# Two passes through a three-batch loop body in place of six written-out batches, on four of five engines

## The reference

```python
x = x + tanh(g_xattn[0]) * xattn(layernorm(x), ctx_512, Wq, Wk, Wv, Wo, bo)
x = x + tanh(g_ffn[0])  * ffn(layernorm(x), gate_w, expert_w, expert_b)

# xattn: 16 heads of 64, keys and values from ctx_512 (8, 512, 128)
scores = einsum('bhnd,bhmd->bhnm', q @ Wq, kv @ Wk) * 64 ** -0.5
out    = einsum('bhnm,bhmd->bhnd', softmax(scores), kv @ Wv) @ Wo + bo

# ffn: softmax router over 8 experts, the two best kept, all experts computed
comb = sum(one_hot(top2(softmax(x @ gate_w.T))) * weight)
out  = sum_e (x @ expert_w[e].T + expert_b[e]) * comb[:, e]
```

## Time and profile before

| | us |
|---|---|
| three timed runs, median | 1011.96 |
| lowest, highest | 1011.67, 1012.37 |
| the profiled execution | 1011.67 |
| its span in the profile | 1009.9 |
| PE busy | 979.5 (97%) |
| DVE busy | 821.2 (81%) |
| ACT busy | 797.1 (79%) |
| POOL busy | 622.4 (62%) |

### The profile page before, as it was taken

The page is one execution under the profiler, slowest core; times in us unless marked ns, Lnnn a source line. Parts: engine busy times, 40 slices in busy tenths (PEclk is TensorE's granted clock), DMA queues, the critical chain, the costliest instruction groups (busy, mean ns, idle before and its releaser), DMA issues.

```text
span 1009.9 us, 27181 instructions
## 1 busy us (share of the span) xinstructions
PE 979.5 (97%) x10656; PEld 770.1 (76%) x10656; DVE 821.2 (81%) x1518; ACT 797.1 (79%) x1404; POOL 622.4 (62%) x371
## 2 busy tenths in 40 slices
PE   7798899999999999999999999999999999999998
PEld 5476777887777877778777787778777787777786
DVE  6577788888888878887888978888788887888768
ACT  5999999777997689886897779977799768987510
POOL 5897777555666557655675746755566655765500
PEclk9899999999999999999999999999999999999999
DMA  4999999787998699995998869977799868998610
GB/s 145 195 205 187 160 182 185 140 128 128 195 166 147 112 161 179 169 151 99 180 169 158 141 115 187 177 138 130 130 190 170 146 110 160 161 154 153 117 35 21
DMA packets 550062, 150.86 MB, mean 149 GB/s; under 512 B 537752, under 2 KB 547376, under 8 KB 549936
## 3 DMA queue, kind: packets, MB, share of 16 engines
q1 hardware_dynamic: 549936, 149.13, 84.7%
HBM read 11.70 MB, written 4.19 MB: 16 GB/s over the span
## 4 chain that ended last, share of the span: by engine, by line
PE 79%; DVE 6%; issue 5%; ACT 4%; POOL 3%; DMA 2%; SPq 0%; ACTq 0%; POOLq 0%; DVEq 0%
PE MB L1076 37%; PE ST L1212 17%; PE PV L1234 16%; PE MB L1088 4%; DVE nmax L873 3%; ACT pf L708 2%; DMA pt_s<-p_s 2%; POOL p_s L552 2%; PE ST L1076 1%; DVE acc L836 1%; PE ST L1243 1%; ACT p_s L718 1%; PE MB L1161 1%; DVE v_s L865 1%; POOL ex_s L590 1%
## 5 line engine op out<-in xcount | busy, mean ns | idle before, releaser
L552 POOL TENSOR_TENSOR p_s<-pf,p_s 128x1024 f16<-128x1024 f32 x254 | 544.3, 2148 | 312.6 <-ACT p_s L718 267.8
L873 DVE TENSOR_REDUCE nmax<-ST 128x2 f32<-128x1024 f32 x256 | 308.4, 1218 | 45.9 <-PE ST L1212 43.0
L708 ACT ACTIVATE pf<-ST,shifts 128x512 f32<-128x512 f32 x512 | 323.8, 688 | 7.6 <-POOL p_s L552 3.7
L718 ACT ACTIVATE p_s<-pf 128x1024 f16<-128x1024 f32 x254 | 267.7, 1060 | 4.2 <-DMA pt_s<-p_s 1.4
L1234 PEld LDWEIGHTS PV<-v_s,pt_s 128*128 128x128 f16 x6096 | 202.2, 98 | 76.7 <-issue 70.4
L1234 PE MATMUL PV<-v_s,pt_s 128*128 128x65 f16 x6096 | 228.8, 194 | 6.4 <-DMA pt_s<-p_s 5.2
L1076 PE MATMUL MB<-ex_s,x2t_s 128*128 128x512 f32 x708 | 189.0, 403 | 0.0
L1076 PEld LDWEIGHTS MB<-ex_s,x2t_s 128*128 128x128 f32 x708 | 126.8, 188 | 24.9
L699 ACT ACTIVATE shifts<-nmax 128x2 f32<-128x2 f32 x256 | 52.8, 206 | 115.8 <-DVE nmax L873 115.3
L836 DVE SCALAR_TENSOR_TENSOR acc<-MB,m,acc 128x256 f32<-128x256 f32 x236 | 113.9, 483 | 29.6 <-PE MB L1076 22.6
L1212 PE MATMUL ST<-KH,QH 64*128 64x512 f32 x512 | 123.0, 476 | 11.4 <-ACT pf L708 8.5
(11 more groups left out here) (141 smaller groups left out, 1047.4 us busy)
## 6 DMA issues: line engine op xcount, KB each, us to landing
pt_s<-p_s SPq DMA_TRANSPOSE x508, 3.4
xin<-x SPq DMA_DIRECT2D x7, 512.0 KB, 4.4
out<-acc SPq DMA_DIRECT2D x7, 512.0 KB, 3.7
kvin<-kv_t SPq DMA_DIRECT2D x8, 256.0 KB, 3.8
acc<-expert_t SPq DMA_DIRECT2D x6, 256.0 KB, 3.5
pf<-wq SPq DMA_DIRECT2D x1, 768.0 KB, 7.2
xin<-x SPq DMA_DIRECT2D x2, 256.0 KB, 2.8
pt_s<-wk SPq DMA_DIRECT2D x1, 512.0 KB, 5.8
```

The source lines that it names most:

```text
L552: pool.tensor_tensor(p_s[:, slot, 1, :, :], pf[:, u % 2, :, :], p_s[:, slot, 0, :, :], ALU.subtract).then_inc(p_lo, 1)
L708: last = act.activation(pf[:, u % 2, i, :], ST[u % 2][:, i, :], ACT.Exp, bias=shifts[:, u % 2, i:i + 1], scale=SCALE)
L718: act.activation(p_s[:, it.ring(p, u, P_SLOTS), 0, :, :], pf[:, u % 2, :, :], ACT.Copy).then_inc(p_hi, 1)
L873: dve.tensor_reduce(nmax[:, t % 2, :], ST[t % 2][:, :, :], AX.X, ALU.max, negate=True)\
```

## The change

`run` gets the engine as an argument. For SP, called with `unrolled=True`, nothing changes. For PE, DVE, ACT and POOL the six middle batches become a hardware loop of two passes. Its body holds three batches, and `it.b` is `n * 3 + (k + 1)` with `n` a register of that engine. So the thresholds of the waits are computed by register instructions in the body, and at its end stand an addition and a compare-and-branch back to its start.

```diff
-        def run(row, before=None, after=None):
+        def run(engine, row, before=None, after=None, unrolled=False):
...
             turn(Iteration(FIRST, 0, 0))
-            for b in range(1, BATCHES - 1):
-                turn(Iteration(LOOP, b, b % LOOPED))
+            if unrolled:
+                for b in range(1, BATCHES - 1):
+                    turn(Iteration(LOOP, b, b % LOOPED))
+            else:
+                with engine.Fori(0, (BATCHES - 2) // LOOPED) as n:
+                    for k in range(LOOPED):
+                        turn(Iteration(LOOP, n * LOOPED + (k + 1), (k + 1) % LOOPED))
             turn(Iteration(LAST, BATCHES - 1, (BATCHES - 1) % LOOPED))
...
-            run(row, before=before, after=after)
+            run(sp, row, before=before, after=after, unrolled=True)
...
-            run(row)
+            run(pool, row)
...
-            run(row, before=before)
+            run(act, row, before=before)
...
-            run(row, before=before)
+            run(dve, row, before=before)
...
-            run(row, before=before)
+            run(pe, row, before=before)
```

## The result

The changed kernel takes 1020.42 us (median; 1015.74 to 1023.04), the kernel before 1012.16 us in the same comparison; the ratio is 1.0079, with a 95% interval of 1.0061 to 1.0095. Timed twice more beside the experiments, the changed kernel gave 1.0073 (1.0057 to 1.0089) and 1.0087 (1.0074 to 1.0100). By the medians it is slower by 8.3, 6.5 and 8.8 us. Its time scatters more than that of before: over 7.3 us here, 3.0 and 3.5 in the two later comparisons, where the kernel before scatters over 1.1, 4.1 and 2.2. The profiled execution took 1018.22 us, with a span of 1016.4: 6.5 us more than the span of before.

What follows compares the result with a forecast made beforehand. PE, busy 979.5 of 1009.9 us, was taken to bound the kernel. Terms of 2.15, 0.85 and 0.6 us, together 3.6, on the profiled 1011.67 us gave 1015.3 us, with a range of 1011.6 to 1025.

Steps and rivals of the forecast that it cites:

- The jump back: Seam between batches 3 and 4: PE stalls 2.15 us, a code load of 2.55 less 0.4 of queued work.
- The cover: At the seam, PE's queued work when its sequencer meets the jump: half the last group of 24 pairs, 0.4 us.
- The other engines' jumps: At the seam, loads of 1.8 us on ACT, DVE and POOL lie beside PE's stall and cost nothing.
- Registers: Wait thresholds computed in the loop bodies: four exposed register instructions a batch, 0.14 us, over six batches 0.85 us.
- Rival C: In every middle batch, register thresholds take PE's time: 1024 us for a third exposed, 1038 for all; chance 0.13.
- Way in and out: Loop entry at 125.4 us and exit at 845.4 us, with an allowance for the compares: 0.6 us at most.
- Rival A: At the seam, PE meets the jump early enough to hide the load: not slower, or 1012 to 1013.6 us; chance 0.25.
- Rival B: At the seam, PE waits for a second load or DVE and ACT resume last: 1018 to 1020 us; chance 0.17.

Runs made afterwards that it cites:

- the announced one: Changed kernel plus one instruction at each loop body's head naming its end jump's target ahead, in both passes; 1019.74 us, 1.0077 to the kernel before.
- the longer cover: Changed kernel with PE's last row reordered, so long matmuls instead of the short `values` stand before the jump; 1020.38 us, 1.0082 to the kernel before.

## Why the prediction was right, and where it was short

The forecast was 1015.3 us and slower; 1020.4 was measured, a cost of 8.3 us where the sum had 3.6. The time is inside the stated range (1011.6 to 1025) because that was wide; it is not inside 1014 to 1017, which the forecast's own mechanism had. The direction, the place and the kind were right: one hole on PE at the seam with packets of both instruction queues in it. The size of the jump's term was not, and the half clock was missing.

- *The jump back, 2.15 us.* It is the step that mattered, and it was mis-sized: 3.50 us of hole in the first trace and 3.73 in the two others. I had priced the load with 2.55 us from the landing of a small store; the jump's record lasts 3.73 to 4.03 us. Its data time was nearly right (1.1, 1.4 and 1.3 us against 1.14), the 1.4 us for everything else was really 2.6 in all three. The cover was 0.6 us where I took 0.4, and 0.35 us from the end of the jump to the first `scores` were in no term: 3.73 - 0.58 + 0.35 = 3.50.
- *What a hole does to the clock* was in no term and in no rival. After each of the seven holes of 2.03 to 3.73 us that a jump or its announcement made on PE (the three profiles of the changed kernel, the loop on PE alone, only PE's jump unannounced, the exit of the announced one, the longer cover) the clock went to 0.50 for 3.4 or 6.8 us; after the two of 1.45 and 1.87 us it did not. The length of one hole does not decide alone: in batch 0 of two profiles a hole of 1.84 and one of 1.85 us were followed by half clock. At the seam this costs 1.0 to 2.2 us in the batch that follows. The earlier trace rows with their clock of 1.00 gave no hint that it could be lost; the start of the program would have. There the kernel before waits 2.46 us, and its clock is down for 6.8 (busy us by engine, then the clock, as above):

```profile
42.99 0.79 PE L1212 MATMUL ST<-KH,QH 64*128 64x512 f32 x2 [2.46 <-ACT pf L708]
42.40:49.20 6.80, 6.21 (x59) 4.65 (x61) 3.75 (x7) 6.67 (x12) 6.80 (x5) 0.50 1.23 222
```

- *The other engines' jumps, nothing.* In the full change they are hidden at the seam, as I wrote, as far as the profiles show: 4.7 and 5.2 us are lost there without them, 5.0, 5.1 and 6.1 with them. The times (1.0054 and 1.0067 without them, 1.0073 to 1.0087 with them) leave room for 1 to 2 us more, whose place I haven't found. Without PE's hole they cost 2.9 us in batch 4, because DVE stands 2.9 us where I had 1.8; I had seen that DVE had no room of its own.
- *Registers, 0.85 us.* Measured 0.5 us over six batches in the run with registers and no jump. Rival C (a cost in every batch, up to 26 us) is refuted by it: 120.0 to 120.1 us a batch.
- *Way in and out, 0.6 us.* The exit costs nothing (164.5 us from batch 7 on in both). Of the entry I can't say more than that batch 1 was longer by 0 to 1.1 us in the kernels with all four loops and by no more than 0.14 in the others.
- *Rival A,* the covered jump, needed a lead of 2.5 us; it was 0.6, and 2.0 with long matmuls ahead of it. *Rival B,* 1018 to 1020 us, came nearest in time. Neither of its mechanisms happened: the next packet of PE's queue comes at 491.56 while PE works, so no second load is in its way, and ACT and DVE are back before PE's first `scores` in all three profiles. That its figure is near is chance.

The Trainium skill, "Runtime: NRT & Kernel Launch", section on instruction fetch mechanics, has the rule that decided: a taken branch outside what is loaded forces a fetch. The run with the jump announced only when taken agrees with it, from 8 us to 1.5. The 64 entries that "Advanced Engine Details and Errata" in the Trainium skill (table of queue depths) gives PE's queue did not show as a lead: when PE met the jump, 27 instructions had yet to start in the changed kernel and 25 in the run with the longer cover.

What stays open: the three profiled executions of the changed kernel are 6.5, 7.0 and 8.1 us longer than that of the kernel before. Of this 5.0, 5.9 and 7.1 us lie in the six middle batches, and 5.0, 5.1 and 6.1 of it at the seam. The rest lies in batch 1 (0, 0.65 and 0.83 us) and in the preparation and batch 0 (1.5, 1.1 and 1.0), where a single profile each of the other kernels doesn't separate the change from chance.

## What to carry to other kernels

A hardware loop with a body as long as these (three batches of a saturated kernel) cost each engine one code load of 2.8 to 4.6 us at the taken jump (PE 3.7 to 4.0), and a saturated TensorE half clock for 3.4 or 6.8 us on top; thresholds from registers cost 0.5 us in six batches. If the loop must stay, announce its jump, and only in the passes in which it is taken (1.0015 against 1.0079 here). Where an engine far from the bound has a jump too, look at who waits for its first instruction behind it.

## What was not expected of the hardware

- A wrong announcement was as dear as none: 1.0077 against 1.0079, with 2.92 us of hole that opened 1.9 us behind a loop's exit.
- How far ahead PE's sequencer got was a matter of instructions, not of time: 27 instructions (14 matmuls, 13 weight loads), 0.6 us of short matmuls, in one kernel, and 25 (13 and 12), 2.0 us of long ones, in the other.
- The half clock came once inside the hole (at 489.8 us, 6.8 us long) and in the six other cases 0.6 to 1.5 us after work had begun again (3.4 us long), so most of it is paid for after the hole is over.
